# Causal attention: one bank for the output accumulator, and the other as a third home of transposed score tiles

## The reference

```python
c_kv = x @ W_kv_down
k = (c_kv @ W_k_up).reshape(Bb, Tt, NH, HD)          # 16 heads of 8
v = (c_kv @ W_v_up).reshape(Bb, Tt, NH, HD)
q = (x @ W_q).reshape(Bb, Tt, NH, HD)
scores = einsum('bqhd,bkhd->bhqk', q, k) + einsum('bqr,bkr->bqk', q_rope, k_rope)[:, None]
scores = where(causal, -inf, scores / sqrt(HD + D_R))  # D_R = 32
w = softmax(scores, axis=-1)
attn = einsum('bhqk,bkhd->bqhd', w, v).reshape(Bb, Tt, D_MODEL)
x = x + attn @ W_o
```

## Time and profile before

| | |
|---|---|
| median of 3 runs | 2027.02 us (2025.97 to 2036.19) |
| the profiled execution | 2027.0 us, which is its span too |
| causal attention | about 120 to 719 us of it |
| TensorE busy in 133 to 719 us | 570.17 of 586 us |
| VectorE, ScalarE busy there | 392.46 and 366.77 us |
| granted TensorE clock there | 1.00 |

### The profile page before, as it was taken

The page is one execution under the profiler, slowest core; times in us unless marked ns, Lnnn a source line. Parts: engine busy times, 40 slices in busy tenths (PEclk is TensorE's granted clock), DMA queues, the critical chain, the costliest instruction groups (busy, mean ns, idle before and its releaser), DMA issues. The chain is left out here.

```text
span 2027.0 us, 40740 instructions
## 1 busy us (share of the span) xinstructions
PE 1782.4 (88%) x15061; PEld 903.7 (45%) x15061; DVE 1410.1 (70%) x3172; ACT 1161.5 (57%) x2314; POOL 581.1 (29%) x817
## 2 busy tenths in 40 slices
PE   5699999999999968799659999999999999777895
PEld 2356666565655545475312222222233332255563
DVE  6676666667788455532669999999899998557431
ACT  3336666666655632232328888888888887332231
POOL 2312122121122146676330000002310000157774
PEclk9779999999999978888769999999999998579798
DMA  5642744553541053232220000000000000062324
GB/s 158 160 81 51 125 84 72 101 90 61 104 81 17 23 143 60 41 53 35 88 110 14 21 17 18 23 27 18 17 18 20 28 5 22 14 168 37 60 38 83
DMA packets 108006, 120.95 MB, mean 60 GB/s; under 512 B 14361, under 2 KB 72961, under 8 KB 107809
## 3 DMA queue, kind: packets, MB, share of 16 engines
q1 hardware_dynamic: 83616, 100.97, 21.1%
q0 software_dynamic: 24192, 17.38, 6.1%
HBM read 81.71 MB, written 35.65 MB: 58 GB/s over the span
## 5 line engine op out<-in xcount | busy, mean ns | idle before, releaser
L1174 DVE TENSOR_REDUCE mx<-wide 128x2 f32<-128x1024 f32 x512 | 604.6, 1220 | 55.2 <-PE wide L1084 42.9
L1208 ACT ACTIVATE pT<-bank 128x512 f32<-128x512 f32 x1024 | 556.8, 596 | 110.9 <-PE bank L1077 102.7
L870 ACT ACTIVATE pT<-bank 128x512 f32<-128x512 f32 (+3 forms) x768 | 350.5, 490 | 248.3 <-PE bank L723 230.0
L1077 PE MATMUL bank<-q_st,k_st 51*128 51x512 bf16 x1024 | 360.4, 397 | 21.0 <-ACT pT L1208 5.2
L1084 PE MATMUL wide<-k_st,q_st 48*128 48x512 bf16 x1024 | 352.6, 399 | 23.6 <-DVE mx L1174 13.9
L1093 PE MATMUL bank<-pT,vst 128*32 128x256 f32 x4096 | 340.2, 405 | 1.8 <-DVEq L1168 1.8
L837 DVE TENSOR_REDUCE mx<-wide 128x1 f32<-128x640 f32 (+3 forms) x256 | 257.2, 1021 | 102.8 <-PE wide L733 97.8
L733 PE MATMUL wide<-k_st,q_st 120*128 120x512 f32 (+3 forms) x768 | 311.1, 417 | 3.5 <-DVE mx L837 1.7
L723 PE MATMUL bank<-q_st,k_st 122*128 122x512 f32 (+3 forms) x768 | 297.8, 392 | 5.5 <-ACT pT L870 3.4
L1793 POOL DMA_INDIRECT acc_rows<-yg,idx x128 | 201.9, 1577 | 105.0 <-DVE yg L2060 71.8
L1077 PEld LDWEIGHTS bank<-q_st,k_st 51*128 51x128 bf16 x1024 | 90.3, 93 | 311.5 <-ACT pT L1208 268.0
(11 more groups left out here) (328 smaller groups left out, 2041.0 us busy)
## 6 DMA issues: line engine op xcount, KB each, us to landing
q_st<-rope_split SPq DMA_DIRECT2D x60, 256.0 KB
k_st<-rope_split SPq DMA_DIRECT2D x60, 256.0 KB
qk_split<-parts SPq DMA_DIRECT2D x8, 1024.0 KB, 6.6
q_st<-qk_split SPq DMA_DIRECT2D x96, 64.0 KB
k_st<-qk_split SPq DMA_DIRECT2D x96, 64.0 KB
qk_parts<-parts SPq DMA_DIRECT2D x8, 768.0 KB, 4.6
xn_rows<-xn SPq DMA_DIRECT2D x8, 512.0 KB, 4.0
w1b<-in_L_ffn_w SPq DMA_DIRECT2D x16, 256.0 KB, 5.2
```

The source lines that it names most:

```text
L870: e.activation(pT[:, u % NPB, q0:HALF], bank[u % 2][:, q0:HALF], ACT.Exp, scale=scale).then_inc(s_p, 1)
L1077: e.matmul(bank[u % 2][:, :], k_st[at][64 * r:64 * r + KROW, jj, kc * P:(kc + 1) * P], q_st[at][64 * r:64 * r + KROW, jj, J * HALF:(J + 1) ...
L1174: e.tensor_reduce(mx[G % 2][:, kh, pair:GH:2, c], wide[w % 2][:, :].rearrange("p (r k) -> p r k", r=2), AX.X, ALU.max).then_inc(s_sf, 1)
L1208: e.activation(pT[:, u % NPB, :], bank[u % 2][:, :], ACT.Exp, scale=scale).then_inc(s_p, 1)
```

## The change

The output accumulator of both halves is bank 2. Bank 3 becomes a third home for tiles, except when it is taken: two steps for each turn (from begins(H+1)+3), and in stacks 8 to 15 from the first lent step to three steps after the last. A table, made when the program is built, gives each tile that bank of the free ones whose last tile is the oldest; a bank last used by a turn or by lent work counts as if used by tile u-3. Each tile waits for what its bank held before: a tile's exponential, a turn's multiplication (`s_y`), or the end of lent work (`s_lent`). The first weighing of a half waits for the copy of the last half's output (`s_oev`); the transposes of a turn wait also for the last tile in their bank.

```diff
-            lent = bank[2][:, :]
+            tiles_in, o_bank, lent = (bank[0], bank[1], bank[3]), bank[2], bank[3][:, :]
+            THIRD = 2
...
+            def third_bank():
+                uses = [(begins(H + 1) + 3, begins(H + 1) + 5, ("turn", H)) for H in range(2 * STEPS)]
+                for s, ats in LENT.items():
+                    uses.append((NP * s + ats[0], NP * s + ats[-1] + 3, ("lent", s)))
+                return sorted(uses)
+
+            def place_tiles():
+                uses, last = third_bank(), [None] * len(tiles_in)
+                at, before, ahead_of_turn = [], [], {}
+                for t in range(LAST + 10):
+                    for begin, _, what in uses:
+                        if begin == t:
+                            if what[0] == "turn":
+                                ahead_of_turn[what[1]] = last[THIRD]
+                            last[THIRD] = what
+                    taken = any(begin <= t < end for begin, end, _ in uses)
+                    for u in (2 * t, 2 * t + 1) if t < LAST else ():
+                        free = [i for i in range(len(tiles_in)) if not (i == THIRD and taken)]
+                        place = min(free, key=lambda i: -1 if last[i] is None else (last[i][1] if last[i][0] == "tile" else u - 3))
+                        at.append(place)
+                        before.append(last[place])
+                        last[place] = ("tile", u)
+                return at, before, ahead_of_turn
+
+            place_of, before_tile, before_turn = place_tiles()
...
+                    def bank_free(used):
+                        if used is None:
+                            return
+                        kind, n = used
+                        if kind == "tile":
+                            e.wait_ge(s_p, PRIME + n + 1)
+                        elif kind == "turn":
+                            e.wait_ge(s_y, PRIME + n + 1)
+                        else:
+                            e.wait_ge(s_lent, n - 7)
+
                     def t_score(u):
                         s, J, kc, j, q0 = unit(u)
                         at = s % NBUF
-                        e.matmul(bank[u % 2][:, q0:HALF], k_st[at][0:KROW, j, kc * P:(kc + 1) * P],
+                        bank_free(before_tile[u])
+                        e.matmul(tiles_in[place_of[u]][:, q0:HALF], k_st[at][0:KROW, j, kc * P:(kc + 1) * P],
...
-                            ins = e.matmul(bank[2 + J][32 * j:32 * (j + 1), qs], vst[s % 2][:, kc, j, :], pT[:, u % NPB, qs],
+                            ins = e.matmul(o_bank[32 * j:32 * (j + 1), qs], vst[s % 2][:, kc, j, :], pT[:, u % NPB, qs],
...
-                            if u >= 2:
-                                e.wait_ge(s_p, PRIME + u - 1)
                             t_score(u)
...
-                            if u >= 2:
-                                e.wait_ge(s_p, PRIME + u)
                             t_score(u + 1)
...
-                            if t - 3 == begins(half_of(t - 3)) and half_of(t - 3) >= 2:
-                                e.wait_ge(s_y, PRIME + half_of(t - 3) - 1)
-                                if half_of(t - 3) % 2 == 0 and half_of(t - 3) // 2 - 1 in LENT:
-                                    e.wait_ge(s_lent, half_of(t - 3) // 2 - 8)
+                            if t - 3 == begins(half_of(t - 3)) and half_of(t - 3) >= 1:
+                                e.wait_ge(s_oev, PRIME + half_of(t - 3))
...
                             e.wait_ge(s_oev, PRIME + H + 1)
+                            bank_free(before_turn[H])
                             for c in range(CPH):
-                                ins = e.transpose(bank[2 + H % 2][:, c * P:(c + 1) * P], o_sb[:, c * P:(c + 1) * P], ident[:, :])
+                                ins = e.transpose(tiles_in[THIRD][:, c * P:(c + 1) * P], o_sb[:, c * P:(c + 1) * P], ident[:, :])
```

More of the change, by code:

```diff
@@ L851, in _ @@
                                 e.wait_ge(s_y, PRIME + H)
-                            o = bank[2 + H % 2][:, :].rearrange("p (c j r) -> p c j r", c=CPH, j=GH)
+                            o = tiles_in[THIRD][:, :].rearrange("p (c j r) -> p c j r", c=CPH, j=GH)
                             e.reciprocal(rsum[:, :, :, :], o[:, :, :, HD:HD + 1]).then_inc(s_ych, 1)
@@ L869, in _ @@
                                     e.wait_ge(s_pv, PRIME + (u // GH - 1) * GH)
-                                e.activation(pT[:, u % NPB, q0:HALF], bank[u % 2][:, q0:HALF], ACT.Exp, scale=scale).then_inc(s_p, 1)
+                                e.activation(pT[:, u % NPB, q0:HALF], tiles_in[place_of[u]][:, q0:HALF], ACT.Exp, scale=scale).then_inc(s_p, 1)
                         if t - 1 in ends:
@@ L875, in _ @@
                                 e.wait_ge(s_ot, PRIME + H)
-                            e.activation(o_sb[:, :], bank[2 + H % 2][:, :], ACT.Copy).then_inc(s_oev, 1)
+                            e.activation(o_sb[:, :], o_bank[:, :], ACT.Copy).then_inc(s_oev, 1)
                         if t - 2 in step_at:
```

## The result

The changed kernel takes 2080.84 us (median of 4 runs, 2073.72 to 2086.29) against 2026.7 us before: a ratio of 1.0251, 95% interval [1.0216, 1.0287]. By that ratio it is slower by 51 us (by the medians 54); 28 were forecast, and the range ended at 2065. The profiled execution spans 2072.0 us.

The account below looks back on a forecast made before the run. TensorE's instruction stream was taken to bound the causal attention, so its waits count in full: 2027.0 - 12.6 (third home) + 39.8 (turn stalls) + 1.0 (lent bank) = 2055.2 us, range 2044 to 2065.

Parts of the forecast that it names:

- the stall: TensorE waiting behind turns for VectorE, which does the turn's multiplication after a reduction: 39.8 us in all.
- The tile named waits for the wait named: Tile 2 of the pair behind a turn waits about 1.9 us for VectorE's multiplication, 22 times.
- the first kind of turn: Turns like the first one, at 139.88 us: the tile behind starts 1.95 us later, eight times.
- the second kind: Turns of a stack's second half: tile 2.0 us later, 1.72 net after 0.19 and 0.10 given back; 14 times, plus one of 0.1.
- The gain: Third home spares tiles waits for exponentials: 1.12 us per stack in 0 to 7, 0.34 in 8 to 15, 12.6 in all.
- lent waits: Tiles waiting for the lent bank a step earlier than weighings did: three cases of 0.15 plus 0.5, 1.0 us.
- the 0.5 of stack 14: Tile at 681.34 us waits for the lent bank until 681.74: 0.4 and the exposed weight load.
- The single accumulator: First weighing of a half waits for the copied output, but 1.76 us of cover hides it: nothing.
- rival C: Stalls at 22 turns lower TensorE's clock: 37 us more (2092) if each does, 2074 if half do; chance 0.08.
- the low case: Idle times of 1.80 and 1.21 us in the profile before, followed by 3.40 us at clock 0.50.
- signs of being wrong: Tile behind the turn not released by VectorE, a stall drawing the clock down, or pairs without waits saving over 0.25 us each.
- half-way: Upper end of the range, set part of the way into rival C, at 2065 us.

Follow-up runs that it names:

- e3_fill6: The changed kernel with six extra matmuls of 512 columns, their results overwritten, ahead of each tile that waits for a turn: 2025.01 us, ratio 1.0121.
- e6_one_acc: The changed kernel with the third home never given to a tile, so one accumulator bank and two homes: 2026.48 us, ratio 0.9994.
- e5_wait_red: The kernel before, with the third tile behind each turn also waiting for the reduction ahead of the turn's multiplication: 2049.76 us, ratio 1.0124.
- e4_wait_y: The kernel before, with the third tile behind each turn also waiting for the turn's multiplication, no bank moved: 2067.24 us, ratio 1.0323.
- e7_fill3: The changed kernel with three extra matmuls ahead of each tile that waits for a turn: 2057.01 us, ratio 1.0151.
- e9_fill1: The changed kernel with one extra matmul ahead of each tile that waits for a turn: 2058.17 us, ratio 1.019.
- e2_turn_first: The changed kernel with VectorE doing a turn's reciprocal and multiplication ahead of the same step's reduction: 1988.51 us, ratio 0.9913.
- e10_first_again: The kernel of e2_turn_first measured again with more rounds, against the kernel before: 2009.59 us, ratio 0.9931.

## Why the prediction was wrong

**The direction, the place and the stall: right.** The tile named waits for the wait named, 22 times, 1.74 to 1.81 us of idle TensorE. By pairs of steps in e3_fill6, where the clock is steady, the pair with the first kind of turn is 1.93 us longer (1.95 forecast), the one with the second kind 1.96 (2.0), and the pair after it 0.26 shorter (0.29).

**The gain: right in the early stacks, to 1.6 us in all.** Over the pairs of an early stack in e3_fill6 the shortenings other than that 0.26 sum to 1.11 us; 1.12 was forecast. Three pairs gained 0.20 to 0.23 where 0.24 stood, three 0.12 to 0.16 where 0.10 stood, a fourth of that kind showed nothing, and two narrow ones gained 0.03 and 0.01 where I had nothing. All stacks: 28.2 forecast with stalls and lent waits, 27.7 measured. Smaller misses cancel in that: stacks 9 to 14 gained about 0.2 each where 0.34 stood, so the whole gain was some 11 us and not 12.6, and the lent bank's waits cost 0.15 in three stacks, while the 0.5 of stack 14 was given back in the pair behind it.

**The single accumulator at nothing: right**, by e6_one_acc.

**The clock: wrong, and it is the whole miss.** The sum has no term for it, and rival C was given 0.08. The failed step is the sentence that weighed it: "against it that in the low case 3.0 of 3.65 us were idle (1460.21 to 1463.85), while here the tiles before and behind the wait are dense". Dense work around the wait did not protect it, and that a stall draws the clock down was one of the prediction's own signs of being wrong. The row for it was there: 1.9 stood nearer to 1.80 than to 1.30, and the price of one stretch, up to 1.7 us, was close to the measured 1.53. What happened is C in a form between its two: 16 low stretches for 22 stalls, 26 us, where "half of them" had been priced at 19 and all at 37. A term or a rival of that size, 2055 + 26 = 2081, was needed. That the measured median is 2080.84 is luck to that decimal: the profiled execution, from which the 26 us are read, spans 2072.0 us, 54 more than before in the stage and 9 less outside it. What the Trainium skill says in "TensorE: Matmul & The Clock Gate", section "A second HAM failure mode: psum-queue depth-cycling", was set aside because short waits had left the clock alone. That stays true of the waits of up to 1.32 us that recur behind the turns (22 of 22 in e5_wait_red); the swing between two clock levels that the section describes is what the 16 low stretches behind the longer ones look like.

**The range: wrong.** Its upper end took C in "half-way" at 2065, 10 us into a case worth 19 to 37, so it neither held C nor left it out by reason. The rest of the range is not quite its own sum either: with a gain of 8 to 20 us and 0 to 8 given back, 2055.2 becomes 2040 to 2060, where 2044 to 2062 was written.

**What stays open.** Why 16 stretches and not 22, and why they come in a pattern that repeats every two stacks (two, one, two, one), is not settled by these runs. Length alone does not sort them: in the changed kernel the clock fell behind 12 of the 14 stalls of 1.74 us and behind only 4 of the 8 of 1.80 and 1.81 us, in e4_wait_y behind 12 of 14 and 3 of 8. Nor is it settled why the part behind the stage is at half clock for 218 us in one trace and for 290 in another, which moves whole times by more than the stage's small gains.

## What to carry to other kernels

A buffer taken back from another engine is free only when that engine gets to it: look at what stands ahead of the release in its queue, and either move the release forward or give the buffer out a few steps later. When an edit adds an idle time to the engine that bounds the kernel, cost the clock with it: find the idle times of that length in the trace, see what the clock did behind each, and give that its own term. And when the time cannot be taken away at once, filler work tells how much of the loss is the wait and how much is the clock.

## What the runs showed of the hardware

Idle times of TensorE that recur in otherwise dense work left the granted clock at 1.00 at 0.98 to 1.04 us (22 times, e7_fill3) and at 1.25 to 1.32 us (22 times, e5_wait_red). At 1.44 to 1.51 us one of 22 was followed by a fall (e9_fill1); at 1.74 to 1.81 us 16 of 22 were in the changed kernel and 15 of 22 in e4_wait_y. Each of these falls lasted 3.4 us or 6.8, at 1.2 GHz, and cost 1.5 us per 3.4 in the dense stacks. The length is not all. In stack 9, where the routing's small matmuls stand between the scores, TensorE idles for 1.3 us in every kernel, and where the clock stays at 1.00 for 1.5 us again 4 us later. Before, nothing followed, nor in seven of the eleven other traces. In e2_turn_first, whose row is below, the clock fell 0.74 us behind the first of the two for 6.8 us (in e10_first_again and e7_fill3 too), and in e6_one_acc 1.76 us behind it for 17.1. A low stretch is also cheaper there: the 6.8 us in e7_fill3 made stack 9 1.5 us longer than in e3_fill6, half the price of the dense stacks.

```profile
471.60 0.22 PE L772 MATMUL wide<-mask_qk,identb 128*128 128x128 bf16 x1 [1.29 <-DVE mx L884]
```

Filling the idle time with matmuls whose results nobody reads kept the clock up and took 26 us off the stage (651.9 to 625.6, e3_fill6).
